# A fourth buffer for VectorE's products and two instead of four for GpSimd's, in a three-layer interaction network

## The reference

```
for W in (W0, W1, W2):
    xk = relu(einsum('bmd,bhd,mhk->bkd', x0, xk, W))
    outs.append(sum(xk, axis=2))
h = concat([outs..., dense_ctx], axis=1)
h = max(h @ W_top1 + b_top1, 0)
h = max(h @ W_top2 + b_top2, 0)
y = h @ W_top3
```

## Time and profile before

| what | value |
|---|---|
| median of 3 runs | 622.93 us (622.63 to 623.33) |
| the profiled execution | 620.85 us |
| its span | 619.1 us |
| PE busy | 562.9 us, 91% |
| DVE busy | 562.7 us, 91% |
| POOL busy | 468.8 us, 76%; idle before gathers 75.0 us, before products 53.2 us |
| ACT busy | 228.1 us, 37% |
| granted TensorE clock | 0.997 of full speed |

### The profile page before, as it was taken

The page is one execution under the profiler, slowest core; times in us unless marked ns, Lnnn a source line. Parts: engine busy times, 40 slices in busy tenths (PEclk is TensorE's granted clock), DMA queues, the critical chain, the costliest instruction groups (busy, mean ns, idle before and its releaser), DMA issues.

```text
span 619.1 us, 7254 instructions
## 1 busy us (share of the span) xinstructions
PE 562.9 (91%) x2752; PEld 203.2 (33%) x2752; DVE 562.7 (91%) x296; ACT 228.1 (37%) x421; POOL 468.8 (76%) x354
## 2 busy tenths in 40 slices
PE   0058789999999999999999999999999999999997
PEld 0012222334333443334333343334333433334334
DVE  0077899999999999999999999999999999999992
ACT  0031605534333534444324434444315434434301
POOL 6748888888888888888888888888888875124450
PEclk9999999999999999999999999999999999999999
DMA  5297979792699819892597819894498819891000
GB/s 170 79 385 252 398 265 397 241 389 65 222 346 325 309 40 375 308 400 91 184 382 295 311 40 376 286 401 142 152 399 282 337 35 344 309 409 77 0 2 0
DMA packets 54245, 151.96 MB, mean 245 GB/s; under 512 B 9697, under 2 KB 18913, under 8 KB 54210
## 3 DMA queue, kind: packets, MB, share of 16 engines
q1 hardware_dynamic: 46018, 149.39, 64.5%
q0 software_dynamic: 8192, 2.11, 2.8%
HBM read 147.26 MB, written 4.20 MB: 245 GB/s over the span
## 4 chain that ended last, share of the span: by engine, by line
PE 68%; DVE 12%; issue 11%; SPq 3%; DMA 2%; ACT 1%; POOL 1%; DVEq 0%
PE acc L536 61%; DVE zd L396 12%; DMA rolled<-x_scratch 2%; PE mlp L578 2%; SPq L277 2%; PE mlp L569 1%; PE mlp L570 1%; PE acc L545 1%; DVE zpart L372 1%; PE mlp L585 1%; PE mlp L552 1%; DVEq L394 0%; POOL zg L325 0%; ACT xk_sb L445 0%; ACT xk_ps L445 0%
## 5 line engine op out<-in xcount | busy, mean ns | idle before, releaser
L396 DVE TENSOR_TENSOR zd<-rolled,xk_ps 128x2048 f32<-128x2048 f32 x239 | 530.6, 2281 | 10.6 <-DMA rolled<-x_scratch 6.5
L536 PE MATMUL acc<-zd,w_sb 128*64 128x512 f32 x1672 | 384.5, 597 | 10.6 <-DVE zd L396 8.5
L313 POOL DMA_INDIRECT emb<-tables_in,index x256 | 244.7, 956 | 75.0 <-issue 64.8
L325 POOL TENSOR_TENSOR zg<-rolled,xk_sb 128x1024 f32<-128x1024 f32 x94 | 223.9, 2383 | 53.2 <-ACT xk_sb L445 19.8
L536 PEld LDWEIGHTS acc<-zd,w_sb 128*64 128x64 f32 x1672 | 116.8, 137 | 251.2 <-issue 228.3
L445 ACT ACTIVATE xk_sb<-acc 64x512 f32<-64x512 f32 x128 | 75.7, 591 | 105.2 <-PE acc L536 90.7
L536 PE MATMUL acc<-zg,w_sb 128*64 128x512 f32 x376 | 97.6, 597 | 3.3 <-POOL zg L325 3.2
L536 PE MATMUL acc<-zd,w 128*64 128x512 f32 x256 | 62.0, 602 | 38.9 <-issue 38.0
L445 ACT ACTIVATE xk_ps<-acc 64x512 f32<-64x512 f32 x126 | 71.8, 570 | 61.6 <-PE acc L536 58.7
L452 ACT ACTIVATE relu_ab<-acc 128x512 f32<-128x512 f32 x48 | 28.7, 597 | 55.5 <-PE acc L536 49.3
L536 PEld LDWEIGHTS acc<-zd,w 128*64 128x64 f32 x256 | 19.2, 138 | 76.7 <-issue 74.4
(11 more groups left out here) (48 smaller groups left out, 76.0 us busy)
## 6 DMA issues: line engine op xcount, KB each, us to landing
rolled<-x_scratch SPq DMA_DIRECT2D x256, 512.0 KB
base<-x_scratch SPq DMA_DIRECT2D x16, 512.0 KB
emb<-tables_in,index POOLq DMA_INDIRECT x256
x_scratch<-emb SPq DMA_DIRECT2D x32, 128.0 KB
w_sb<-w_in SPq DMA_DIRECT2D x2, 512.0 KB
wt<-wtop_in SPq DMA_DIRECT2D x1, 512.0 KB
wt1a<-wtop_in SPq DMA_DIRECT2D x1, 256.0 KB
w<-w0a_in SPq DMA_DIRECT2D x1, 160.0 KB
```

What stands on the lines that cost most here:

```text
L313: pool.indirect_dma_start(emb[:, i % 2, c * DIM:(c + 1) * DIM], None, tables, bass.IndirectOffsetOnAxis(index[:, g:g + 1].bitcast(U32), 0) ...
L325: nc.gpsimd.tensor_tensor(zg[:, n % ZG_BUFS, :], rolled[:, s, j, :], xk_sb[:, s, :], ALU.mult).then_inc(zg_ready, 1)
L396: nc.vector.tensor_tensor(zd[:, n % ZD_BUFS, 0:w, :], rolled[:, s, j:j + w, :], repeated(layer_in, w), ALU.mult).then_inc(zd_ready, 1)
L536: end = nc.tensor.matmul(acc[h * MAPS:(h + 1) * MAPS, s, :], weights, z[:, h * HALF:(h + 1) * HALF], start=(j + c == 0), stop=(i == len(me ...
```

## The change

It gives DVE's products four buffers of two chunks instead of three, and POOL's products two buffers of one chunk instead of four. The memory is the same in all (a DVE buffer is twice as large). No instruction is added, removed or reordered; the modulus of the buffer index and the count in the two waits change: DVE product n now waits for PE to have finished DVE product n - 4 (before n - 3), and POOL product n for PE to have finished POOL product n - 2 (before n - 4).

```diff
-ZD_BUFS = 3
-ZG_BUFS = 4
+ZD_BUFS = 4
+ZG_BUFS = 2
```

## The result

The changed kernel takes 628.95 us (median of 4 runs, 627.80 to 629.62) against 623.13 us for the kernel before (now the median of 4 runs, 622.63 to 624.90): the ratio is 1.009, with a 95% interval of 1.0069 to 1.0111. It is slower by 5.8 us; 630.2 us was forecast, 7.3 us above the 622.93 us known then, in a range of 624.5 to 636. In the later runs (e8) it took the same 628.95 us, at a ratio of 1.0083 (1.0067 to 1.0099). The profiled execution of the changed kernel took 629.62 us, its span 627.8 us.

What follows compares the result with a forecast made beforehand. DVE and PE were taken as nearly full, POOL as running without a pause on a lead used up at product 69. Lateness of 9.3 us less 1.75 us regained adds 7.5 us to 622.93: 630.4, written 630.2 us, range 624.5 to 636.

Steps and rivals of the forecast that it cites:

- POOL's pushes: POOL products 9, 14 and 16, waiting for the release two back, start 2.6, 5.7 and 6.3 us later.
- PE late at product 21: POOL product 21 ends at 193.1 us, PE wants it at 190.16: PE is 3.0 us late.
- The loop: From product 21 to 69, PE and POOL hold each other, 72.05 us per pair, four times; PE 9.3 us late at 69.
- What is worked off: After product 69 PE regains 1.75 us of its lateness, wherever it idled before.
- POOL's margin: After product 69 POOL waits for releases but stays about 1.6 us ahead of PE with two buffers.
- The sum: End moves by 9.3 - 1.75 = 7.5 us; on the median 630.4 us, written as 630.2; chance 0.68.
- The fourth DVE buffer: Removes DVE's waits for PE's release, 0.7 us per pair, 4.4 us at most, if everybody else keeps up.
- DVE's waits: DVE's waits for PE move from inside the products after 222 us to one per pair of 1 to 3 us.
- PE's waits for POOL: Grow from 3.2 us in two to some 12 to 15 us in ten or more, largest at products 21, 33, 45, 57, 69.
- The rival of the loads: SP's last rolled loads, waiting for POOL's product, land late and delay DVE in some five pairs: 645 us; chance 0.07.
- The rule that was weighed: DVE's repeated gap means too few buffers; by that alone the fourth buffer saves 4.4 us: 618.5 us; faster 0.08.

Runs made afterwards that it cites:

- e8: The changed kernel measured again, unchanged, beside the other runs: 628.95 us, ratio 1.0083 to the kernel before.
- e3: Changed kernel with two gathers per pair moved into the stretch of POOL products 28 to 33, list equally long: 641.59 us, ratio 1.0307 to the kernel before.
- e4: Changed kernel with two gathers per pair moved out of the stretch of POOL products 28 to 33, list equally long: 623.82 us, ratio 1.0020 to the kernel before.
- e1: Kernel before with two POOL buffers instead of four, DVE's three kept: 630.56 us, ratio 1.0137.
- e5: Changed kernel with two gathers per pair fewer among POOL products 28 to 33, six made up behind product 71: 619.26 us, ratio 0.9934 to the kernel before.
- e7: Kernel before (three DVE, four POOL buffers) with only the two gather lines of e5: 623.81 us, ratio 1.0008.
- e6: Kernel before with two POOL buffers, three DVE buffers and the two gather lines of e5: 624.60 us, ratio 1.0019.
- e2: Kernel before with three POOL buffers instead of four, DVE's three kept: 623.11 us, ratio 1.0009.

## Why the prediction was right

**POOL's pushes.** Product 9 was to be pushed by 2.6 us, 14 by 5.7 and 16 by 6.3; with the later start taken off they are pushed by 2.6, 5.7 and 6.3 us (for 16: 167.18 - 159.24 - 1.65). The wait went where it was named, behind products 7, 12 and 14.

**PE late at product 21.** Forecast 3.0 us; 194.78 against 190.16, less 1.65, is 3.0.

**The loop.** Forecast 72.05 us per pair, measured 71.95 to 71.99 in four pairs. Its two long terms are right as well: PE from product 21 to the release of 26 was to take 44.3 us (194.78 to 239.06), and POOL from there to PE's start on 33 27.7 us (239.06 to 266.74). It is shown to be a loop by e3 and e4, which lengthen or open it with the same instructions. PE is 9.0 us late at product 69 (forecast 9.3): 482.66 - 472.04 - 1.65.

**What is worked off.** Forecast 1.75 us. Without the later start taken off, PE takes product 93 8.8 us later than before and took product 69 10.6 us later: 1.85 us. POOL's margin there is right too: it was to stay about 1.6 us ahead of PE, and at product 76 its product is done 1.66 us before PE takes it.

**The sum.** The two profiled executions differ by 8.8 us, 7.1 us without the later start; forecast 7.5. The medians differ by only 5.8 us, so the sum is 1.7 us above what the change costs in the median. The execution profiled before was 2.3 us below its median and the one after 0.7 us above its own. Part of that is the start: in the ten traces of this case PE takes product 9 at 119.5 to 122.3 us, and the kernel before is the earliest, 1.4 us ahead of the middle one of the others. What makes up the rest stays open: a PE that is late anyway may swallow small waits that the kernel before pays in its slower executions, but no run shows it.

**The fourth DVE buffer.** That it gives nothing while POOL holds PE was nearly right: 1.6 us (e1), most of which arises behind product 69, where POOL holds PE no longer. That it could give 4.4 us, if everybody else keeps up, is borne out where POOL isn't in the way: 4.6 us (e5 against e7, though e5 has two POOL buffers and e7 four). Beside two POOL buffers it gives 5.3 us (e5 against e6); the 0.8 us between the two is within the noise, and in a pair it is the 0.45 us of e7.

**Where I was wrong in a detail.** DVE's waits were to move to one per pair of 1 to 3 us for PE. In fact the wait is split: 0.7 us ahead of the product that needs PE's release, and in the pair from 266.73 us 0.6, 0.5 and 0.3 us ahead of reductions, which wait for ACT, which waits for the late PE (the longest of the 13, 5.7 us, is in the filling):

```profile
269.58 2.29 DVE L396 TENSOR_TENSOR zd<-rolled,xk_ps 128x2048 f32<-128x2048 f32 x1 [0.71 <-issue]
...
295.67 0.69 DVE L372 TENSOR_REDUCE zpart<-relu_ab 128x32 f32<-128x512 f32 x1 [0.63 <-ACT relu_ab L452]
```

```profile
DVE zpart L372 <- ACT relu_ab L452: 11.4, 13, 5.7
```

The total over a pair is 2.1 us (71.96 less 69.84 us of work), within the 1 to 3 that were forecast. PE's waits for POOL were forecast at 12 to 15 us in ten or more; they are

```profile
PE acc L536 <- POOL zg L325: 13.7, 16, 1.8
```

The longest, 1.8 us, is in the filling; then come those at products 21, 33, 45, 57 and 69 with 1.64 to 1.69 us, as forecast.

**The rival of the loads.** SP's rows for the streams of the earlier trace rows:

```profile
302.97 17.08 SPq L277 DMA_DIRECT2D rolled<-x_scratch  x16
...
328.52 0.52 SPq L268 DMA_DIRECT2D base<-x_scratch  x1
```

The 16 loads take 4.1 us longer to issue, as they wait for POOL's products, but base follows 25.6 us after the first of them (26.7 before); less the later start it is issued only 0.2 us later than before. It costs nothing: behind the filling the view names one wait of DVE of more than 0.2 us for rolled chunks,

```profile
198.09 2.29 DVE L396 TENSOR_TENSOR zd<-rolled,xk_ps 128x2048 f32<-128x2048 f32 x1 [0.41 <-DMA rolled<-x_scratch]
```

and none of 0.05 us or more from there to product 69. That a late issue finds a backlog of transfers, as the prediction argues, fits this, but no run separates it.

**The rule that was weighed.** DVE's repeated gap did come from too few buffers, as the Trainium skill (Perfetto Trace Analysis, Optimization Strategy) suggests. The trace agrees where POOL isn't in the way: with a fourth buffer the gap of 0.48 us is gone and a pair takes 69.51 instead of 70.19 us (e5 against e7). The 618.5 us that the rule alone would give were missed by 10 us, since here the memory was taken from POOL, which then held PE.

## What to carry to other kernels

Before taking a buffer from a producer, compare its start with the release one buffer sooner, product by product, and set the push against the leads that come later. A push below the lead of the first product at which a loop could close costs about itself where the lead runs out, and in e2 nothing that the medians show; above it, the lateness grows with each turn of the loop (e1). A producer that looks idle can be the one with no slack: POOL is busy for 87% of a pair before and 76% of the whole, and the rest of the pair is the pauses at its gathers. Once two engines hold each other through two buffers, the work that stands between release and delivery counts in full. Moving two gathers to the other side of the wait took back nearly the whole loss, to 1.0 us above the kernel before (e4); the buffer bought for DVE paid only when two gathers per pair were taken off POOL's list as well (e5).

## What was not expected of the hardware

The loop repeats to 0.04 us over four pairs, and the same kernel in the later runs (e8) gives 72.00 us, while whole executions of it spread by 1.8 us (627.8 to 629.6 us). A good part of such a spread can arise before the first pairs: PE takes POOL product 9 at 119.52 us in the trace of the kernel before, and between 119.59 and 122.33 us in the nine others, with no order by the number of buffers (e3 and e4, both with four and two, have 119.59 and 121.77). There is one trace for each run, so how much of the spread of a kernel comes from there isn't shown.
